# Context groups and integer weights turned by DMA instead of TensorE in a two-layer cross-attention and FFN kernel

## The reference, cut to what matters

```python
x = x + xattn(layernorm(x), ctx, Wq0, Wk0, Wv0, Wo0, bo0)      # 32 batches, 256 rows, width 256
x = x + ffn(layernorm(x), w_gate, w_up, w_down)                # int32 weights * (1/127), hidden 768
x = x + xattn(layernorm(x), ctx, Wq1, Wk1, Wv1, Wo1, bo1)
x = x + int8_product(layernorm(x), rhs)                        # rows and rhs quantised to int8

def xattn(x, ctx, Wq, Wk, Wv, Wo, bo):                         # 16 heads of 64; ctx is 32 x 77 x 192
    k, v = ctx @ Wk, ctx @ Wv                                  # 2464 context rows in all
    return softmax(q @ k.T / 8) @ v @ Wo + bo

def ffn(x, wg, wu, wd):
    return (silu(x @ wg.T) * (x @ wu.T)) @ wd.T                # wg, wu: 768 x 256; wd: 256 x 768
```

## Time and profile before

| | |
|---|---|
| median of 3 runs | 1627.0 us (1626.41 to 1629.02) |
| the profiled execution: its own time | 1625.34 us |
| its span, first to last instruction | 1623.5 us |
| granted TensorE clock, mean | 0.995 |
| TensorE busy | 1560.3 us, 96% |
| VectorE, ScalarE, GpSimd busy | 84%, 85%, 78% |
| first part: first matmul of tile (0,0) to that of the last tile | 12.29 to 207.65 us |

### The profile page before, as it was taken

The page is one execution under the profiler, slowest core; times in us unless marked ns, Lnnn a source line. Parts: engine busy times, 40 slices in busy tenths (PEclk is TensorE's granted clock), DMA queues, the critical chain, the costliest instruction groups (busy, mean ns, idle before and its releaser), DMA issues.

```text
span 1623.5 us, 74775 instructions
## 1 busy us (share of the span) xinstructions
PE 1560.3 (96%) x27354; PEld 1446.7 (89%) x27354; DVE 1357.6 (84%) x3519; ACT 1379.5 (85%) x5665; POOL 1271.7 (78%) x1892
## 2 busy tenths in 40 slices
PE   7999978999999999999999999999999999999995
PEld 4555668999999999999999999999999999999994
DVE  5777757888888888888888887888898889888985
ACT  5665678899998998998999988889999999999993
POOL 4200068899999999998999888788999999999994
PEclk9999999999999999999999999999999999999998
DMA  8975689987887777778778989899999889989995
GB/s 253 327 275 223 221 183 175 160 176 173 176 177 178 168 174 182 166 177 176 171 172 179 173 172 161 153 178 197 191 201 198 189 190 200 198 190 190 196 191 104
DMA packets 732250, 305.82 MB, mean 188 GB/s; under 512 B 621424, under 2 KB 717584, under 8 KB 730064
## 3 DMA queue, kind: packets, MB, share of 16 engines
q1 hardware_dynamic: 730272, 297.29, 83.4%
q0 software_dynamic: 1840, 6.82, 1.3%
HBM read 87.72 MB, written 65.54 MB: 94 GB/s over the span
## 4 chain that ended last, share of the span: by engine, by line
PE 36%; POOL 31%; issue 11%; DVE 5%; DMA 2%; ACT 1%; SPq 1%; POOLq 0%; ACTq 0%; DVEq 0%
PE psum L308 27%; POOL pr L1486 9%; POOL p L1493 8%; POOL p L1489 6%; PE psum L1115 5%; POOL rs L368 3%; POOL hT_l L1476 3%; PE psum L306 2%; PE psum L299 2%; DVE oT_l L337 1%; DMA pT<-p 1%; DVE x L1465 1%; POOL y L1514 1%; POOL x_res L1502 1%; DMA x2T<-x 1%
## 5 line engine op out<-in xcount | busy, mean ns | idle before, releaser
L1230 ACT ACTIVATE ex<-psum,nmax 128x77 f32<-128x77 f32 x2048 | 638.0, 335 | 44.4 <-DVE nmax L1347 35.7
L1230 ACT ACTIVATION_READ_ACCUMULATOR ex<-psum,nmax 128x1 f32 x2048 | 443.3, 216 | 0.0
L1493 POOL TENSOR_TENSOR p<-pr,p 128x308 f16<-128x308 f32 x512 | 413.2, 807 | 38.4
L1486 POOL TENSOR_TENSOR pr<-ex,rden 128x308 f32<-128x308 f32 x512 | 369.8, 722 | 57.7 <-DVE rden L1352 57.1
L308 PE MATMUL psum<-xT,wq_h 128*64 128x256 f16 x4064 | 348.7, 273 | 0.0
L1347 DVE TENSOR_REDUCE nmax<-psum 128x4 f32<-128x308 f32 x512 | 241.1, 471 | 56.2 <-PE psum L308 53.8
L308 PE MATMUL psum<-xT,wq_l 128*64 128x256 f16 x2032 | 283.5, 273 | 0.0
L1489 POOL CAST p<-pr 128x308 f16<-128x308 f32 x512 | 242.3, 473 | 42.9 <-DMA pT<-p 10.7
L308 PE MATMUL psum<-kb,qT_h 128*64 128x154 f16 x4096 | 261.0, 231 | 11.5 <-DVE qT_l L340 4.1
L308 PE MATMUL psum<-wo_h,oT_h 128*64 128x256 f16 x1792 | 251.1, 275 | 15.2 <-DVE oT_l L337 14.5
L308 PE MATMUL psum<-wo_l,oT_h 128*64 128x256 f16 x1792 | 249.8, 273 | 0.0
(11 more groups left out here) (159 smaller groups left out, 3554.7 us busy)
## 6 DMA issues: line engine op xcount, KB each, us to landing
keys<-ks SPq DMA_DIRECT2D x16, 1232.0 KB, 5.2
kb<-keys SPq DMA_DIRECT2D x256, 77.0 KB, 2.8
vb<-vals SPq DMA_DIRECT2D x128, 154.0 KB
vals<-vs SPq DMA_DIRECT2D x64, 256.0 KB, 3.1
x_pair<-in_x_dram SPq DMA_DIRECT2D x32, 256.0 KB, 3.0
pT<-p SPq DMA_TRANSPOSE x512, 3.3
x_res<-in_x_dram SPq DMA_DIRECT2D x32, 256.0 KB, 3.0
mid_x<-y SPq DMA_DIRECT2D x32, 256.0 KB, 2.4
```

Of the source, the lines that this page charges most:

```text
L1230: last = act.activation(ex[i][:, t, b, :], SC[:, t, b * NK:(b + 1) * NK], ACT.Exp, bias=nmax[i][:, t, b:b + 1], accum_out=den[i][:, t, b:b ...
L1486: pool.tensor_tensor(pr[:, t, :, :], ex[i][:, t, :, :], r, ALU.mult).then_inc(s_p, 1)
L1493: pool.tensor_tensor(d[:, t, 1, :, 0:NK], pr[:, t, :, :], d[:, t, 0, :, 0:NK], ALU.subtract).then_inc(s_pl, 1)
```

## The change

1. For groups 1 to 3 the context is loaded in one piece by two DMAs (`load_group`), split in its own layout (rows on partitions), and turned as float16 by one DMA transpose of 128 x 1920 (`turn_group`), which brings high, low and the last 64 features at once. Its destination `ct` replaces `c0h`, `c0l` and `c1`. The split is a cast and a subtraction of 128 x 640 behind tile 29, and of 128 x 320 behind tile 33 (`split_group`). Group 0 stays as it was.
2. The six integer pieces are cast straight to float16 (`convert`), in the order that the turn wants, and turned by DMA into `wgT`, `wuT` and `wdT` (`turn_weights`; two DMAs for a piece of `w_gate` or `w_up`, one for a piece of `w_down`).
3. TensorE loses `turn_half` 2 to 7 and `turn_ints`; ScalarE loses `copy_turned`. TensorE waits for `s_ctd` ahead of tile (i,0) of groups 1 to 3, and once for `s_wd` ahead of the second part.

```diff
-        raw_f = [raw_f2[:, i * HID:(i + 1) * HID] for i in range(2)]
+        raw_16 = raw_f2[:, :].bitcast(F16)
+        w16 = [raw_16[:, i * HID:(i + 1) * HID] for i in range(4)]
...
+        cx_all = sb("cx", [P, 2 * 3 * 2 * P], F32, early)
+        cx = [cx_all[:, i * 6 * P:(i + 1) * 6 * P].rearrange("p (t c) -> p t c", t=3) for i in range(2)]
+        cg = cx_all[:, 0:VR * DC].rearrange("p (t c) -> p t c", t=VR)
+        cx16 = sb("cx16", [P, 3, VR, P], F16, early)
+
+        ct = [sb(f"ct{i}", [P, 3, VR * P], F16, early) for i in range(2)]
+        c0h, c0l, c1 = ([ct[i][:, k, :] for i in range(2)] for k in range(3))
...
-        TURN_INT_AT = {(i, j + 2): k for (i, j), k in CONVERT_AT.items()}
-        INT_AT = {(i, j + 3): k for (i, j), k in CONVERT_AT.items()}
...
-        TURN_AT, SPLIT_AT = {29: 0, 37: 1}, {31: 0, 39: 1}
+        WEIGHTS_AFTER = {(1, 0, 2): 0, (1, 0, 3): 1, (1, 1, 4): 2, (2, 0, 0): 3, (2, 0, 3): 5}
+        SPLIT_AT = {29: 0, 33: 1}
...
+                def load_group(g):
+                    t1 = (VR - 1) * P
+                    src = ctx_t[g * GRP:(g + 1) * GRP, :]
+                    sp.dma_start(cg[:, 0:VR - 1, :], src[0:t1, :].rearrange("(t p) c -> p t c", p=P)).then_inc(s_cg, 16)
+                    sp.dma_start(cg[0:GRP - t1, VR - 1, :], src[t1:GRP, :]).then_inc(s_cg, 16)
+
+                def turn_group(g):
+
+                    sp.wait_ge(s_cgl, 2 * g)
+                    after(sp, s_kv, (g - 1) * KVT)
+                    sp.dma_start_transpose(ct[g % 2][:, :, :].rearrange("p r (t q) -> p (r t) q", q=P),
+                                           cx16[:, :, :, :].rearrange("p r t c -> p (r t c)")).then_inc(s_ctd, 16)
+
+                def turn_weights(j):
+
+                    sp.wait_ge(s_int, j + 1)
+                    dsts = turned[j][1]
+                    n = HID // len(dsts)
+                    for k, dst in enumerate(dsts):
+                        sp.dma_start_transpose(dst, w16[j % 4][:, k * n:(k + 1) * n]).then_inc(s_wd[j], 16)
...
-                        for n in range(2, 4):
-                            sp.wait_ge(s_ct, 2 * n - 2)
-                            load_half(n)
+                        sp.wait_ge(s_ct, 4)
+                        load_group(1)
...
                 for i in range(NG - 1):
                     if 1 <= i:
-                        for n in (2 * i + 2, 2 * i + 3):
-                            sp.wait_ge(s_ct, 2 * n - 2)
-                            load_half(n)
+                        sp.wait_ge(s_cgl, 2 * i)
+                        load_group(i + 1)
                     for l in range(2):
                         for half in range(2):
                             store_keys(i, l, half)
+                            if l == 1 and half == 0:
+                                turn_group(i + 1)
+                            if i == 2 and l == 0 and half == 1:
+                                turn_weights(4)
                         for t in range(VR):
                             store_values(i, l, t)
+                            if (i, l, t) in WEIGHTS_AFTER:
+                                turn_weights(WEIGHTS_AFTER[i, l, t])
...
+                def split_group(g, part):
+
+                    if part == 0:
+                        act.wait_ge(s_cg, 32 * g)
+                        after(act, s_ctd, 16 * (g - 1))
+                        act.activation(cx16[:, 0, :, :], cg[:, :, 0:P], ACT.Copy).then_inc(s_cgh, 1)
+                    else:
+                        act.activation(cx16[:, 2, :, 0:DCR], cg[:, :, P:DC], ACT.Copy).then_inc(s_cgh, 1)
...
-                def copy_turned(j):
-                    act.wait_ge(s_wt, j + 1)
-                    for k, o in enumerate(turned[j][2]):
-                        src = psum[:, 6 + k, 0:3 * P]
-                        if len(o.shape) == 3:
-                            src = src.rearrange("p (t d) -> p t d", d=P)
-                        act.activation(o, src, ACT.Copy).then_inc(s_wte, 1)
...
+                def split_group(g, part):
+
+                    dve.wait_ge(s_cgh, 2 * (g - 1) + part + 1)
+                    if part == 0:
+                        low(dve, cx16[:, 1, :, :], cg[:, :, 0:P], cx16[:, 0, :, :]).then_inc(s_cgl, 1)
+                    else:
+                        low(dve, cx16[:, 2, :, DCR:P], cg[:, :, P:DC], cx16[:, 2, :, 0:DCR]).then_inc(s_cgl, 1)
...
                 def convert(j):
 
                     dve.wait_ge(s_ri[j], 16)
-                    if j < 2:
+                    if j < 4:
                         dve.wait_ge(s_kp, 3)
                     else:
-                        dve.wait_ge(s_wt, j - 1)
-                    dve.tensor_copy(raw_f[j % 2], int_land[:, j, :]).then_inc(s_int, 1)
+                        dve.wait_ge(s_wd[j - 4], 16 * len(turned[j - 4][1]))
+                    o, i = w16[j % 4], int_land[:, j, :]
+                    if len(turned[j][1]) == KT:
+                        o = o.rearrange("p (k t q) -> p k t q", k=KT, q=P)
+                        i = i.rearrange("p (t k q) -> p k t q", k=KT, q=P)
+                        for k in range(KT):
+                            last = dve.tensor_copy(o[:, k], i[:, k])
+                    else:
+                        last = dve.tensor_copy(o, i)
+                    last.then_inc(s_int, 1)
...
-                        pe.wait_ge(s_cl, 2 * (2 * i + b) + 2)
+                        if i == 0:
+                            pe.wait_ge(s_cl, 2 * b + 2)
+                        elif b == 0:
+                            pe.wait_ge(s_ctd, 16 * i)
...
-                def turn_ints(j):
-                    pe.wait_ge(s_int, j + 1)
-                    if j >= 1:
-                        pe.wait_ge(s_wte, 2 * j)
-                    for c, k, t in turned[j][1]:
-                        last = pe.transpose(psum[:, 6 + k, t * P:(t + 1) * P],
-                                            raw_f[j % 2][:, c:c + P], ident[:, :])
-                    last.then_inc(s_wt, 1)
...
-                        if i < NG - 1 and j in TURN_AT:
-                            turn_half(2 * i + 2 + TURN_AT[j])
-                        if (i, j) in TURN_INT_AT:
-                            turn_ints(TURN_INT_AT[i, j])
...
+                for j in range(NT):
+                    pe.wait_ge(s_wd[j], 16 * len(turned[j][1]))
```

More of the change, by code:

```diff
@@ L166, in xattn_ffn_kernel @@
         s_int = sem("s_int")
-        s_wt = sem("s_wt")
-        s_wte = sem("s_wte")
         s_wh = sem("s_wh")
@@ L197, in xattn_ffn_kernel @@
                 src = w[a * 3 * P:(a + 1) * 3 * P, :].rearrange("(t p) d -> p t d", p=P)
-                blocks = [(t * D + k * P, k, t) for k in range(KT) for t in range(3)]
-                turned.append((src, blocks, [wT[:, k, a * 3 * P:(a + 1) * 3 * P] for k in range(KT)]))
+                turned.append((src, [wT[:, k, a * 3 * P:(a + 1) * 3 * P].rearrange("p (t q) -> p t q", q=P)
+                                     for k in range(KT)]))
         for a in range(KT):
-            src = w_down[a * P:(a + 1) * P, :]
-            blocks = [(c * P, c // 3, c % 3) for c in range(HC)]
-            turned.append((src, blocks, [wdT[:, 3 * k:3 * k + 3, a * P:(a + 1) * P] for k in range(2)]))
+            turned.append((w_down[a * P:(a + 1) * P, :], [wdT[:, :, a * P:(a + 1) * P]]))
         NQO, NT = len(qo_items), len(turned)
@@ L209, in xattn_ffn_kernel @@
         s_ct = sem("s_ct")
+        s_cg, s_cgh, s_cgl, s_ctd = sem("s_cg"), sem("s_cgh"), sem("s_cgl"), sem("s_ctd")
+        s_wd = [sem(f"s_wd{j}") for j in range(6)]
         s_ch = sem("s_ch")
@@ L571, in _ @@
                         if i < NG - 1 and j in SPLIT_AT:
-                            split_half(2 * i + 2 + SPLIT_AT[j])
-                        if (i, j) in INT_AT:
-                            copy_turned(INT_AT[i, j])
+                            split_group(i + 1, SPLIT_AT[j])
                         if (i, j) in QO_AT:
@@ L753, in tile_product @@
                     last.then_inc(s_kv, 1)
-                def turn_ints(j):
-                    pe.wait_ge(s_int, j + 1)
-                    if j >= 1:
-                        pe.wait_ge(s_wte, 2 * j)
-                    for c, k, t in turned[j][1]:
-                        last = pe.transpose(psum[:, 6 + k, t * P:(t + 1) * P],
-                                            raw_f[j % 2][:, c:c + P], ident[:, :])
-                    last.then_inc(s_wt, 1)
                 def turn_rhs():
                     pe.wait_ge(s_rr, 16)
-                    pe.wait_ge(s_cl, 4 * NG)
+                    pe.wait_ge(s_cl, 4)
                     for t in range(KT):
```

1 line of the change is left out of this document (removed).

## The result

The changed kernel takes 1646.2 us (median of four runs, 1642.2 to 1650.2) against 1626.7 us before: 1.012 times as long, with a 95% interval of 1.009 to 1.015. The forecast was 1619.8 us, range 1615.8 to 1626.0. The prediction is wrong by 26 us, and in sign: it forecast a faster kernel and this one is slower. The profiled execution took 1642.2 us, of which 1640.4 are the span; it is the fastest of the four.

A forecast was written before the change was run, and what follows sets the result against it. TensorE was taken to bound the first part; -10.7 (its work) + 2.5 (group 1 turn) + 0.4 (VectorE) + 0.3 (later turns) + 0.3 (added waits) = -7.2 from 1627.0, giving 1619.8 us, range 1615.8 to 1626.0.

The forecast's parts named there:

- the second part begins when TensorE is through, and its own work is unchanged: First part: a microsecond taken from TensorE's list there should come off the end.
- nothing by themselves: ScalarE: the copies of the turned weights leave it, and since it is not the bound this gains nothing.
- Its own sign of being wrong: Profile after: prediction wrong if the first part's 7 us shift is lost in the second part.
- slower rival: Turns: small-packet transposes get little of full engines, waits of 10.4 and another 11 us, about 1639 us; chance 0.06.
- TensorE's work: First part: six context halves (6.4 us) and six integer pieces (4.3 us) leave TensorE, together 10.7 us less.
- The turn of group 1: Ahead of tile (1,0): turn lands at 62.5, TensorE waits 2.5 us, bounds 0 and 6.0.
- the upper bound taken for it: Group 1 turn's own time behind the store: 8.0 us, with half of the engines' time lost to POOL's loads.
- Waits for VectorE: First part: new split costs TensorE waits, old waits of 0.7 us go; net loss 0.4 us, bounds -0.7 and +1.5.
- its upper bound: VectorE in groups 1 and 2: still late from a weight split at tile 24, waits up to 0.8 us there.
- Waits ahead of the second part: Ahead of the second part: six more waits, all long met, put at 0.3 us (0 to 0.6).
- The turns of groups 2 and 3: Ahead of tiles (2,0) and (3,0): second turn just in time, third has room; 0.3 us, bounds 0 and 4.
- The rate of a turn: DMA transpose of 128 x 1920: 3.8 us for its data, scaled from 2.04 us for 128 x 1024.

The follow-up runs named there:

- experiment 1: Changed kernel with 28 increments of an unused semaphore ahead of ScalarE's first cast, moving its loop back to 726: 1614.6 us, ratio 0.993 to the kernel before.
- 3: Kernel before with only the context split in its own layout and turned by DMA, integers left on TensorE, 16 increments keeping the loop at 726: 1620.9 us, 0.997.
- 6: Changed kernel with 16 increments ahead of ScalarE's first cast, its loop at 714: 1651.7 us.
- 8: Changed kernel without increments, ScalarE's first loop holding one pass in place of two (143 instructions, start 698): 1619.1 us, 0.996 of the kernel before.
- experiment 5: Changed kernel with 8 increments ahead of ScalarE's first cast, its loop at 706: 1660.6 us.
- experiment 11: Changed kernel with one-pass loop, no increments, POOL's first loads moved away from the first turn, two weight splits two tiles earlier: 1616.7 us, 0.994 of the kernel before.
- 4: Kernel before with only the integer weights cast to float16 and turned by DMA, context left on TensorE, 12 increments keeping the loop at 726: 1622.9 us, 0.998.
- 12: Kernel before with only POOL's loads moved, as a control: 1626.6 us, 0.999 of the kernel before.
- experiment 7: Changed kernel padded by 28 increments, the next group's context turn issued ahead of the key store instead of behind it: 1621.3 us, 0.996 of the kernel before.

## Why the prediction was wrong

The step that failed is the sentence on which every microsecond was carried to the end: "the second part begins when TensorE is through, and its own work is unchanged". Its work is unchanged, but not the place of its instructions in ScalarE's program. 28 instructions fewer ahead of a loop of 280 made eleven jumps back wait 2.6 us each: 28.1 us of waits on ScalarE and 3.6 us of shorter ones a few instructions further on, of which 25.9 reached the end (in the profiled executions; the medians with and without the increments of experiment 1 lie 31.7 us apart). This was no term and no rival. The prediction put ScalarE's lost copies at "nothing by themselves", since ScalarE is not the bound, and did not ask what their absence does to the code behind them. Its own sign of being wrong, a shift that is lost in the second part, is what came. The prediction's slower rival gave a number near the result (1639) by another mechanism: that nearness is luck, and experiment 1 shows that this was not the cause.

In the first part the sum held, though not each of its terms:

- *TensorE's work*, -10.7: borne out within 0.4 us. From tile (0,0) to the second part there are 8.6 us less, and -10.7 with the waits measured below gives -8.2. The integers alone gave 4.3, net of 0.3 for the new waits ahead of the second part.
- *The turn of group 1*: a landing "some 16 us after its issue" was forecast, 15.9 was measured:

```profile
L397 SPq DMA_TRANSPOSE ct<-cx x1: 11491/11491/11491, 45.0 to 45.0; - x1
...
DMA to landing us min/median/max: 15.9/15.9/15.9
```

  and the key store ahead of it:

```profile
L432 SPq DMA_DIRECT2D keys<-ks x1: 343/343/343, 44.6 to 44.6; - x1
...
DMA to landing us min/median/max: 8.3/8.3/8.3
```

  The turn landed at 45.0 + 15.9 = 60.9 for 62.5, and the wait was 1.36 us for 2.5. That the landing came out so near is in part luck, for two terms were off against each other: the store landed at 52.9 and not at 58.0, and the turn 8.0 us behind it and not 4.5, as much as the upper bound taken for it. In experiments 1, 3, 6 and 8, which leave turn, store and loads in place, the wait was 0.9, 0.8, 1.1 and 1.9 us; experiment 5, which leaves them in place too, had 8.4. That there would be one wait at this place was right, and POOL's loads were rightly named beside it; its spread is at the upper end larger than the bound of 6.0. What decides between some 16 and some 23 us for the same transfer stays open. The prediction also took 1.26 us of issue for a turn, where SyncE was held for 11.5 us and the next key store went out at 56.5.
- *Waits for VectorE*, +0.4: +0.8 (4.2 us against the 3.4 of the earlier trace rows). The waits of the earlier trace rows went, and two of 0.71 came at (1,30) and (2,30), with the cause that the prediction named for its upper bound (experiment 11).
- *Waits ahead of the second part*, +0.3: 2.15 us against 1.83 before.
- *The turns of groups 2 and 3*, +0.3: no wait. The store ahead of the second turn landed in 11.2 us (10.6 forecast) and the turn 12.9 us after the store's issue (14.4); the third turn landed in 6.8, under 10 as forecast. ScalarE waited for no store in the first part.
- *The rate of a turn.* Each turn is issued less than 0.5 us behind a store of 1232 KB, so its 15.9, 12.4 and 6.8 us hold the store too. The third was issued at 136.2, with no load of POOL's beside it, and landed 2.4 us behind its store (143.0 against 140.6); by the same count the second took 1.7 and the first 8.0. The forecast's 3.8 us for a turn's own data lies between. By the figure of the Trainium skill (Advanced Engine Details and Errata, X-Bar Transpose) it would be 1.3 us, an estimate; the trace shows more at each of the three, and a wait at tile (1,0) where there would have been none.

With the loop in a good place the changed kernel is at 1614.6 us, 11.5 us under the kernel before (interval 8.6 to 14.5), below the forecast of 1619.8 and the low end of its range, 1615.8. Of the 11.5 us, 8.4 lie in the first part. The rest is of the size by which the second part differs from run to run where nothing in it was changed (in experiment 8, only ScalarE's loop): from its first matmul to the end of the span it took 1408.1 us in experiment 1, 1411.8 and 1416.7 in 3 and 4, 1413.4 in 8 and 1415.5 in 12. I don't claim it for the change. With the loop of one pass and no increments the changed kernel is at 1619.1 us, the forecast within a microsecond.

Two things were not tried: a loop on another engine that crosses a border, and a loop of just 256 instructions, so that the length from which a place can be bad is worked out and not measured (280 can be bad, 143 was not at the same start).

## What to carry to other kernels

An edit ahead of a hardware loop moves the loop in its engine's program. Where the loop is long (here 280 instructions on ScalarE; by the theory anything over a block of 256), compare its start before and after; shorten the loop (here to 143), or pad it to a good place found by a run, before you judge the edit by its time. This is shown for ScalarE alone. In a profile the sign is a wait for "issue" on the first instruction behind a jump, once a round, and an instruction queue with many more packets: look there whenever a part that the edit doesn't touch has become slower.

## What the hardware showed that I had not expected

- In a loop of 280 instructions on ScalarE, a jump back waits some 2.5 us, up to 3.3, when the loop starts at 698, 706 or 954, and not at 726. At 714 a second wait follows each jump (26.7 and 21.5 us in eleven jumps).
- SyncE is held while a large transpose is issued: 11.5, 9.6 and 4.3 us for three turns of equal size, where a store of 1232 KB mostly takes 0.34 us to issue. Stores can hold it too: one of 1232 KB took 4.39 us to issue in experiment 11.
- A transpose beside POOL's loads slows both: in experiment 7 the engines show a share over 1 and move 102 to 152 GB/s, and the load of the third integer piece lands in 15.1 us for 6.5 before. The first turn, 480 KB, lands 15.4 to 23.4 us after its issue; where those loads are gone 10.5 to 11.3, and in group 2, with nothing beside it but its own queue, 6.8.
- An increment of a semaphore on ScalarE takes about 0.07 us: 28 of them move its first table load from 0.74 to 2.63 us.
